# Inner attention scores over each head's own 32 rows, maxima of two heads in two banks, new step lists

## The reference

```python
q = _rope(split(c @ wq), pos)          # 16 heads of width HD = 4
k = _rope(split(c @ wk), pos)
v = split(c @ wv)
scores = jnp.einsum('bhqd,bhkd->bhqk', q, k) / jnp.sqrt(jnp.float32(HD))
causal = jnp.tril(jnp.ones((s, s), bool))
scores = jnp.where(causal, scores, -jnp.inf)
attn = jax.nn.softmax(scores, axis=-1)
o = jnp.einsum('bhqk,bhkd->bhqd', attn, v).transpose(0, 2, 1, 3).reshape(b, s, L)
x = x + o @ w_up
```

## Time and profile before

| what | value |
|---|---|
| time, median of 3 runs | 705.74 us |
| span of the profiled execution, first to last instruction (the page gives no other time of it) | 704.1 us |
| PE busy, instructions | 623.6 us (89%), 5090 |
| DVE busy, instructions | 510.4 us (72%), 1712 |
| ACT busy, instructions | 409.8 us (58%), 794 |
| POOL busy, instructions | 344.8 us (49%), 390 |
| mean granted TensorE clock, as a share of full speed | 0.972 |

### The profile page before, as it was taken

The page is one execution under the profiler, slowest core; times in us unless marked ns, Lnnn a source line. Parts: engine busy times, 40 slices in busy tenths (PEclk is TensorE's granted clock), DMA queues, the critical chain, the costliest instruction groups (busy, mean ns, idle before and its releaser), DMA issues.

```text
span 704.1 us, 15681 instructions
## 1 busy us (share of the span) xinstructions
PE 623.6 (89%) x5090; PEld 409.6 (58%) x5090; DVE 510.4 (72%) x1712; ACT 409.8 (58%) x794; POOL 344.8 (49%) x390
## 2 busy tenths in 40 slices
PE   8987699999999989999998999898978887999980
PEld 3434356556646655564665556455445577899970
DVE  7364967787896888789688878767777456357994
ACT  3234256566556656655665665456525675688971
POOL 4043265158158455815845581444401457567782
PEclk9999999999999999999999999999989999999995
DMA  5201001000110100010010001001511114236652
GB/s 170 78 0 31 1 1 30 2 1 1 35 32 1 31 31 6 1 39 26 2 31 30 6 1 43 24 2 32 188 29 34 48 57 117 84 94 181 173 162 87
DMA packets 40219, 34.19 MB, mean 49 GB/s; under 512 B 6673, under 2 KB 37329, under 8 KB 40129
## 3 DMA queue, kind: packets, MB, share of 16 engines
q1 hardware_dynamic: 35824, 23.84, 12.7%
q0 software_dynamic: 4320, 9.38, 3.9%
HBM read 17.54 MB, written 12.57 MB: 43 GB/s over the span
## 4 chain that ended last, share of the span: by engine, by line
PE 40%; DVE 22%; POOL 18%; issue 12%; ACT 3%; DMA 2%; SPq 1%; DVEq 0%; POOLq 0%; ACTq 0%
DVE nmax L1411 7%; PE small L866 5%; PE wide L886 4%; PE small L911 4%; PE wide L1101 4%; PE small L898 3%; POOL result_rows L1349 3%; PE small L934 3%; PE small L963 3%; DMA result_rows<-k_rows,dest 2%; PE small L870 2%; POOL k_rows L1324 2%; PE wide L891 2%; DVE a_xn L1403 2%; DVE a_st L1392 2%
## 5 line engine op out<-in xcount | busy, mean ns | idle before, releaser
L1411 DVE TENSOR_REDUCE nmax<-small 128x1 f32<-128x512 f32 (+3 forms) x352 | 216.3, 636 | 49.7 <-PE small L870 46.8
L1198 ACT ACTIVATE pT<-wide 128x1024 f32<-128x1024 f32 x160 | 159.2, 1022 | 58.1 <-PE wide L891 57.1
L866 PE MATMUL small<-kz,qT 128*128 128x256 bf16 (+3 forms) x512 | 125.4, 306 | 13.5 <-DVE nmax L1411 13.0
L1340 POOL DMA_INDIRECT token_rows<-m_row,place_u x64 | 62.8, 981 | 118.4 <-DVE place_u L1625 89.4
L886 PE MATMUL wide<-qT,kz 128*128 128x512 bf16 (+3 forms) x512 | 97.6, 304 | 9.5 <-DVE qT L1562 7.9
L1349 POOL DMA_INDIRECT result_rows<-k_rows,dest x71 | 69.3, 976 | 39.0 <-issue 19.7
L870 PE MATMUL small<-future_sb,idb 128*128 128x128 bf16 (+2 forms) x352 | 87.2, 248 | 0.0
L911 PE MATMUL small<-pT,v_pad 128*5 128x512 f32 (+3 forms) x1024 | 76.5, 438 | 0.8 <-issue 0.7
L866 PEld LDWEIGHTS small<-kz,qT 128*128 128x128 bf16 x512 | 44.1, 98 | 48.3 <-DVE nmax L1411 30.6
L886 PEld LDWEIGHTS wide<-qT,kz 128*128 128x128 bf16 x512 | 43.9, 99 | 43.3 <-issue 11.7
L1752 DVE TENSOR_TENSOR a_work<-a_work,wide 128x256 f32<-128x256 f32 x71 | 29.7, 418 | 39.1 <-ACT a_work L1230 15.2
(11 more groups left out here) (250 smaller groups left out, 1285.7 us busy)
## 6 DMA issues: line engine op xcount, KB each, us to landing
a_qkv_sb<-token_rows SPq DMA_DIRECT2D x71, 72.0 KB, 1.9
kz<-k_all SPq DMA_DIRECT2D x32, 128.0 KB, 2.4
x<-L_attn_x SPq DMA_DIRECT2D x8, 256.0 KB, 3.9
kz<-L_ffn_w SPq DMA_DIRECT2D x2, 1024.0 KB, 7.4
kz<-result_rows SPq DMA_DIRECT2D x16, 128.0 KB, 2.3
out<-x SPq DMA_DIRECT2D x16, 128.0 KB
result_rows<-k_rows,dest POOLq DMA_INDIRECT x71, 2.2
token_rows<-m_row,place_u POOLq DMA_INDIRECT x64
```

Source lines behind the costliest of these rows:

```text
L866: pe.matmul(bank[:, at:at + keys], qT1[:, m.parity, g, tile * P:(tile + 1) * P], kz[:, m.parity, g, r, 0:keys], start=(r == r0), stop=Fals ...
L1198: act.activation(pT[:, g % 2, s, :], wide[:, w % 2, :], ACT.Exp, scale=SCALE_B)\
L1340: pool.indirect_dma_start(token_rows[:, :], bass.IndirectOffsetOnAxis(ap=place_u[:, n, t:t + 1], axis=0), m_row[:, n, t, :], None).then_in ...
L1411: ins = dve.tensor_reduce(nmax[:, tile, g * R + r0:g * R + r0 + heads], bank[:, 0:heads * (tile + 1) * P].rearrange("p (h k) -> p h k", h= ...
```

## The change

Keys are kept turned but not padded (`kT`, both batch parities; `kz`, `k_all`, the transfers of p_rows and `clear_keys` go). A head's score product takes its own 32 rows as contraction. Masks are still products over 128 rows and now come first in a bank; the head products accumulate onto them. A maxima job has two heads, one in bank 0 and one in bank 1, and holds both; six jobs a group instead of eleven, the last two with two reductions. An exponential job has two heads, one per bank of `wide`; six a group instead of five, two of them with 512 columns and four with 1024. Of a maxima and an exponential job joined by `&` in PE's list, all masks are issued first and then the products of the four heads in turn. The expert weights and two result buffers that lay over `kz` get memory of their own. The step lists of the nine iterations between the first and the last are written anew.

```diff
-MAX_JOBS = [(3, r, 1) for r in range(R)] + [(2, r, 1) for r in range(R)] + [(1, 0, 2), (1, 2, 2), (0, 0, R)]
-PT_AT = {0: 0, 1: 512, 3: 896}
-EXPS = R + 1
+MAX_JOBS = [(((3, 0),), 0), (((3, 0),), 1), (((2, 0),), 0), (((2, 0),), 1), (((1, 0), (0, 2 * P)), 0), (((1, 0), (0, 2 * P)), 1)]
+EXP_JOBS = [(((0, 0),), 0), (((0, 0),), 1), (((1, 0), (3, 3 * P)), 0), (((1, 0), (3, 3 * P)), 1), (((2, 0),), 0), (((2, 0),), 1)]
+EXPS = len(EXP_JOBS)
...
     "PE": """
-        m_x1_0 f_pv2 m_shift0 m_x1_1 m_x1_2 m_e00 m_e01 f_o1 m_x1_3 m_e02 m_x1_4 m_e03 m_x1_5 f_pv3 a_xT
+        f_pv2 m_shift0 m_x1_0 f_o1 f_pv3 m_x1_1&m_e00 m_e01 a_xT f_o2 m_x1_2 a_qkv0 a_qkv1 m_x1_3 a_qkv2 a_qkv3
...
     def bank(self, job):
-        return self.index(job) % 2 + (0 if is_max(job) else 2)
+        return 0 if is_max(job) else 2 + self.index(job) % 2
...
-                        for r in range(R):
-                            sp.dma_start(kz[32 * r:32 * r + 32, p.parity, :, r, :],
-                                         k_all[32 * r:32 * r + 32, :, :]).then_inc(kz_in, 16)
...
+            def head_rows(r):
+                return slice(32 * r, 32 * r + 32)
+
+            def max_masks(m, ring, g, n):
...
+                for i in range(2):
+                    pe.matmul(small[:, i, lo:lo + len(blocks) * P], idb[:, :], future_sb[:, 0:len(blocks), :],
+                              start=True, stop=False, skip_group_check=True)
...
+            def max_product(m, g, n, block, i):
+                blocks, pair = MAX_JOBS[n]
+                rows = head_rows(2 * pair + i)
+                tile, at = blocks[block]
+                keys = keys_up_to(tile)
+                return pe.matmul(small[:, i, at:at + keys], qT1[rows, m.parity, g, tile * P:(tile + 1) * P],
+                                 kT[rows, m.parity, g, 0:keys], start=False, stop=True, skip_group_check=True)
...
+            def scores(ring, p, m, step):
...
+                for job in exps:
...
+                    exp_masks(*job)
+                for of, g, n in maxima:
+                    max_masks(of, ring, g, n)
+                for block in range(2):
+                    for job in exps:
...
+                            last = exp_product(*job, block, i)
...
+                    for of, g, n in maxima:
...
+                            last = max_product(of, g, n, block, i)
...
-                ins = dve.tensor_reduce(nmax[:, tile, g * R + r0:g * R + r0 + heads],
-                                        bank[:, 0:heads * (tile + 1) * P].rearrange("p (h k) -> p h k", h=heads),
-                                        AX, ALU.max, negate=True)
+                for tile, at in blocks:
+                    ins = dve.tensor_reduce(nmax[:, tile, heads], small[:, 0:2, at:at + keys_up_to(tile)],
+                                            AX, ALU.max, negate=True)
```

More of the change, by code:

```diff
@@ L147 @@
+        p_x2 p_x3 a_r p_x4 a_rstat p_x5 m_o0""",
     "POOL": """
         p_x1 a_rstd p_rstd p_rs a_ropeq a_ropek p_rope p_cut p_slots a_rrstd""",
[L149 to L150 removed]
 }
@@ L233, in is_max @@
 def is_max(job):
-    return job[1:3] == "_x"
+    return job[1:3] == "_x" and job != "a_xT"
 def max_name(g, n):
@@ L241, in jobs @@
 def jobs(stages):
-    return [s for s in steps(stages, "PE") if "_e" not in s and s[:4] not in ("warm", "tile", "plan")]
+    parts = [j for s in steps(stages, "PE") for j in s.split("&")]
+    return [j for j in parts if j[1:3] != "_e" and j[:4] not in ("warm", "tile", "plan")]
 NTOK = NB * T
@@ L586, in jobs_before @@
             maxima = sum(map(is_max, before))
-            return [(n // 2, n % 2) for n in (maxima, len(before) - maxima)]
+            others = len(before) - maxima
+            return [(maxima, 0), (others // 2, others % 2)]
         def iterations(eng, body):
@@ L885, in exp_job @@
-                for r, tile, at in blocks:
-                    pe.matmul(bank[:, at:at + T - tile * P], kz[:, m.parity, g, r, tile * P:(tile + 1) * P],
-                              qT2[:, g % 2, tile * P:T], start=(at % T == 0), stop=False, skip_group_check=True)
-                for diagonal in diagonals:
-                    n = 1 if len(diagonal.shape) == 2 else 2
-                    last = pe.matmul(diagonal, idb[:, :], future_T[:, 0:n, :] if n > 1 else future_T[:, 0, :],
-                                     start=False, stop=True, skip_group_check=True)
@@ L893, in exp_job @@
-                last.then_inc(wide_full[w % 2], 1)
+                for i in range(2):
+                    bank = wide[:, w % 2, i * T:(i + 1) * T]
+                    diagonal = bank.rearrange("p (n k) -> p n k", k=P)[:, 0:NT:3, :] if len(blocks) > 1 else bank[:, 0:P]
+                    pe.matmul(diagonal, idb[:, :], future_T[:, :, :] if len(blocks) > 1 else future_T[:, 0, :],
+                              start=True, stop=False, skip_group_check=True)
+            def max_product(m, g, n, block, i):
+                blocks, pair = MAX_JOBS[n]
+                rows = head_rows(2 * pair + i)
[3 more added lines that the diff above has]
+                                 kT[rows, m.parity, g, 0:keys], start=False, stop=True, skip_group_check=True)
```

263 lines of the change are left out of this document (114 added, 149 removed).

## The result

The changed kernel takes 728.21 us (median of 4 runs, 723.56 to 730.79) against 705.3 us for the kernel before (4 runs, 704.15 to 705.88) on the same chip: a ratio of 1.0317, 95% interval [1.0274, 1.0361]. It is 3% slower; 692 was forecast, and the range ended at 717.

The account below looks back on a forecast made before the run. PE was taken to set the pace, busy 58.8 of 61.6 us in a full iteration. Full iterations +3, other iterations -12.4 and beginning -3.7 gave -13 us: 692 us, forecast case 683 to 703, whole range 668 to 717.

Parts of the forecast that it names:

- PE's part: TensorE work per full iteration: fewer columns -8.8 and -1.8, shape changes +8.5, weight loads +2.0, sum -0.1 us.
- the joined step: Sign on PE, masks to next start: 0.85 us if right, 0.6 if shape change is cheap, 1.3 if heads queue.
- the change of shape: PE switching the array's row shape in and out: about 0.23 us a step, 37 steps, 8.5 us per full iteration.
- heads don't overlap: Rival on PE's score products: 10.6 us an iteration come back, 770 us; chance 0.05.
- cheaper: Rival: shape change cheaper, 0.1 us a step, or waits go; full iterations 58.5 us, 675 us in all; chance 0.22.
- The single slot's charge: Maxima job holding both banks, so PE cannot fill while DVE reduces: 0.7 us of waits per full iteration.
- single-slot rival: DVE and PE take turns: 713 us, chance 0.23; signs: full iterations 64.5 us and more, PE waits for nmax over 5.
- The clock falls: Rival: full iterations drop to a clock like `mf`'s 0.90, 3 to 6 us more each, 715 us; chance 0.05.
- The other iterations: Less full iterations with new lists, PE's busy share rising to 0.95: `apm` -2.1, `pmf` -4.7, `mf` -5.6, together -12.4 us.
- DVE's part: Reductions fall from 44 to 32 an iteration: 1.9 us of DVE less, by itself worth nothing.
- The beginning: Zeroing of `kz` gone, -0.7 us; second iteration's maxima no longer late, first m_cut at 76 us, -3 us.
- The tail: Expert tiles and routing behind the iterations, 151 us, whose lists stay: must not move.

Follow-up runs that it names:

- padded version: Changed kernel's jobs, slot and lists, but products over all 128 rows with zero-padded keys: 756.07 us, 1.074 against the kernel before; on a slower chip 820.46 us, 1.075.
- version c: Changed kernel with exponential masks twice in every step and m_x3_0's masks six times: 719.52 us, 1.020 against the kernel before; on a slower chip 804.28 us, 1.057.

## Why the prediction was wrong, step by step

**PE's part: right in mechanism, too dear in the sum.** Heads overlap (starts 0.01 apart, forecast 0.05), the joined step took 0.76 to 0.78 (0.85), the single x job 0.55 (some 0.6), the change of shape 0.22 (0.23). The rival "heads don't overlap" is out, and so is "cheaper" at its 0.1 a step. But a few hundredths in each of 37 steps add up: PE is busy 56.2 us in the full iteration at 1.00, 2.6 less than before (58.8), where 0.1 less was forecast.

**The single slot's charge (0.7 an iteration): too small.** PE stands idle 5.6 us of that iteration (61.8 less 56.2), for 2.8 before: 2.8 more. DVE waits 6.9 us for maxima products there (4.2 in the earlier trace rows). PE's waits were worked out up to 15.7 us of the list; the longest pause lies 30 us in. So the 61.8 us, against a forecast of 62, are two errors of nearly one size that cancel, which is luck. The signs of the single-slot rival came in half: the mean iteration has 64.9 us (64.5 and more), but PE's weight loads wait 3.6 and 2.7 us for maxima reductions in the first two, not over 5.

**"The clock falls (0.05)": the step that failed.** The sum left the full iterations at a clock of 1.00; they ran at 1.00, 0.85, 0.97, 0.92 and 0.92. Full iterations cost 17.2 us more, for +3, and 15.4 of them stand above five times the iteration at full clock. The rival's price, 3 to 6 us an iteration, holds the mean of 3.4 (17.2/5), but it had a chance of 0.05, from one row, `mf` at 0.90 "where PE had idle stretches". That reading was right: the kernel before falls behind pauses. Two things were not asked: where the new list gathers its waits (1.7 us idle in 3, for 1.1 before), and what products of 32 rows do to the clock, which PE shows as just as busy. The sum took columns for the whole cost. With 128-row products the clock held behind 1.6 us of idle in 3 (padded version); with 32-row ones it fell behind 0.3 to 1.7.

**"The other iterations" (-12.4): failed.** `apm` -0.8, `pmf` +2.7, `mf` +2.3. PE's share was to rise to 0.95; in `pmf` it is 49.3 of 58.5, 0.84, and it was 0.87. The waits of `pmf`, before:

```profile
PEld small L866 <- DVE nmax L1411: 7.5, 11, 2.2
DVE nmax L1411 <- PE small L870: 5.5, 9, 1.3
```

and after:

```profile
DVE nmax L1402 <- PE small L857: 13.1, 17, 3.4
PEld small L839 <- DVE nmax L1402: 8.8, 11, 1.4
```

Both wait, in turn: this is the single slot, not in the full iterations for which the rival had priced it, but where less other work stands between two maxima. At a clock of 0.94 it is still there (version c: 15.2 and 8.8 of the same two waits). So a part is the slot or the list, a part the clock (0.88 and 0.77 in the last two). For `mf` one run tells them apart: at the same clock as before (0.90), with exponential masks twice in joined steps, it takes 49.1 us for 52.0. There the new list gains some 3 us, and the clock takes them away. For `pmf` how much is which stays open.

**DVE's part: near.** 216.3 - 204.8 = 11.5 us of reductions less over the run, and worth nothing by itself.

**The beginning (-3.7): -1.4.** The rotary starts at 12.62 for 13.19, as forecast; the first cut is at 78.2, not 76.5 (79.64 in the earlier trace rows). **The tail: 152.6 for 151**, at a clock of 0.92 for 0.94; the forecast said it must not move, and it moved by 1%.

In numbers: -13 was forecast, +21.6 came. Full iterations account for 14 of the difference (+17.2 for +3), the other iterations for 16.6 (+4.2 for -12.4), beginning and tail for 3.9.

## What to carry to other kernels

Count for each TensorE product not only its columns but how many of the array's rows it uses: where a change packs small products, also ask what the granted clock will do, and try the new mix as a stretch by itself before rebuilding the kernel. Go through the whole list for the place where waits gather: a pause that the old work bore can be too long for the new. A buffer slot that is safe in the fullest iteration is to be tried in the emptiest, where nothing stands between filling and emptying. Put iterations of one code with different lengths side by side, and the row of the clock tells whether the difference is the clock's. Where a sum hits an iteration, check its terms too: two of them can cancel.

## What the runs showed of the hardware

- The granted clock falls from 1.00 to 0.50 while PE is recorded busy without a gap, when the work is 32-row products of 512 columns in one strip, or units of two 128-column masks and a pair of 256 or 128 columns. The Trainium skill (TensorE: Matmul & The Clock Gate, Part 1: The HAM clock gate) says that activity releases the throttle and names waits as what brings it back. The traces agree for most falls, such as all five in the padded version's full iterations; the runs add that a busy row in the profile is not yet enough.
- In full iterations falls stood behind 2.1 us or more of PE idle in 3 where all scores were 128-row products, and behind 0.3 to 1.8 us, too, where some were 32-row ones.
- Four row strips of 512 columns ran in 0.217 us a four, a full fourfold of 0.217 for one. The same page (Part 3, Measured speedup) gives 3.07 times; here the measurement decides.
- Exponential masks issued twice in joined steps made the kernel 1.6% faster (729 to 717 us on one chip).
- On the slower chips one place of every full iteration was stretched. Windows of the changed kernel there, around the eight token sends of POOL:

```profile
430.51:433.92 3.41, 1.70 (x17) 0.85 (x14) 0.96 (x1) 1.82 (x3) 2.50 (x4) 1.00 0.22 67
433.92:437.34 3.42, 1.03 (x8) 0.77 (x8) 0.69 (x1) 0.27 (x1) 2.51 (x4) 0.58 0.13 46
437.34:440.75 3.41, 1.41 (x10) 0.91 (x10) 1.48 (x3) 0.94 (x2) 0.94 (x1) 0.50 0.14 43
```

PE, DVE and ACT are idle for most of it, and the iteration takes 72.8 us. What holds them is open: the waits name a releaser that the trace doesn't show.
